# Split parts moved from GpSimd to VectorE ahead of layer 0, and an aggregation ordered by source tile

## What is computed

```python
h = maximum(layernorm(x), 0);  x1 = x + h              # x_in = h
g = batch_norm(h over the nodes) * bn_w + bn_b
g = gcn(g, gcn_in_w)      # out[d] = sum over edges s->d and s = d of (g @ W)[s] * dinv[s] * dinv[d]
for i in range(4):        # layers
    g = g + cross_attention(ln(g), cond, Wq, Wk, Wv, Wo)
    g = g + (val * gelu(gate)) @ ffo_w,  val, gate = split(ln(g) @ geglu_w)
g = gcn(g, gcn_out_w)
return x1 + g
```

## Time and profile before

| | |
|---|---|
| median of 3 runs | 2732.07 us |
| the profiled execution's own time | 2735.34 us |
| its span, first to last instruction | 2733.5 us |
| TensorE matmul busy | 2532.7 us, 93% |
| VectorE busy | 1371.1 us, 50% |
| ScalarE busy | 900.6 us, 33% |
| GpSimd busy | 762.6 us, 28% |
| first matmul of layer 0 | 364.14 us |
| share of the chain that ended last | PE 84%, DVE 10% |

### The profile page before, as it was taken

One profiled execution on the slowest core, in us unless ns is written; L12 is line 12 of the kernel. 1 busy time (PEld: TensorE's weight loads), 2 busy tenths in 40 slices (PEclk: granted clock), 3 DMA queues, 4 the chain that ended last, 5 costly groups with the idle time before them and its releaser, 6 DMA issues.

```text
span 2733.5 us, 34690 instructions
## 1 busy us (share of the span) xinstructions
PE 2532.7 (93%) x12399; PEld 2071.0 (76%) x12399; DVE 1371.1 (50%) x2852; ACT 900.6 (33%) x1735; POOL 762.6 (28%) x550
## 2 busy tenths in 40 slices
PE   2665779999999999999999999999999999999999
PEld 1231568888888788888888788888887888888887
DVE  9989636665222366663222566642223666622233
ACT  4132233335322133344222233352222333442211
POOL 4126220002544200015443000035442000154431
PEclk6576889999999999999999999999999999999999
DMA  3151331110221111111112011102111111011251
GB/s 130 43 219 77 138 128 38 56 77 16 77 64 67 74 62 62 36 47 64 65 66 96 32 62 61 47 31 78 62 65 63 62 62 77 16 62 62 69 205 68
DMA packets 39441, 197.48 MB, mean 72 GB/s; under 512 B 4112, under 2 KB 4496, under 8 KB 27024
## 3 DMA queue, kind: packets, MB, share of 16 engines
q1 hardware_dynamic: 39312, 195.81, 19.3%
HBM read 166.43 MB, written 29.36 MB: 72 GB/s over the span
## 4 chain that ended last, share of the span: by engine, by line
PE 84%; DVE 10%; issue 2%; DMA 1%; POOL 1%; ACT 1%; SPq 0%; POOLq 0%; ACTq 0%; DVEq 0%
PE ps L1286 25%; PE ps L1287 25%; PE ps L1288 25%; DVE oh_d L976 2%; PE ps L1449 2%; DVE oh_s L1015 2%; DVE oh_d L1017 2%; PE ps L1466 2%; PE ps L1468 2%; PE ps L1463 1%; DMA stage<-in_pieces 1%; DVE oh_s L974 1%; DVE z L1193 1%; PE ps L1490 1%; PE ps L1476 1%
## 5 line engine op out<-in xcount | busy, mean ns | idle before, releaser
L1286 PE MATMUL ps<-xT_hi,wg_hi 128*128 128x512 f32 (+1 forms) x1088 | 416.5, 383 | 0.0
L1287 PE MATMUL ps<-xT_lo,wg_hi 128*128 128x512 f32 (+1 forms) x1088 | 414.7, 381 | 0.0
L1288 PE MATMUL ps<-xT_hi,wg_lo 128*128 128x512 f32 (+1 forms) x1088 | 414.7, 381 | 0.0
L1240 DVE SCALAR_TENSOR_TENSOR ff<-ps,cols_sb,gel 128x512 f32<-128x512 f32 x128 | 96.1, 750 | 594.0 <-ACT gel L795 594.0
L795 ACT ACTIVATE gel<-ps,cols_sb 128x512 f32<-128x512 f32 x128 | 88.2, 689 | 637.9 <-PE ps L1288 637.8
L1249 DVE TENSOR_TENSOR h<-h,ps 128x512 f32<-128x512 f32 x256 | 175.6, 686 | 148.1 <-PE ps L1288 148.1
L1288 PEld LDWEIGHTS ps<-xT_hi,wg_lo 128*128 128x128 f32 x1088 | 209.8, 193 | 37.5
L1286 PEld LDWEIGHTS ps<-xT_hi,wg_hi 128*128 128x128 f32 x1088 | 210.0, 193 | 37.3
L1287 PEld LDWEIGHTS ps<-xT_lo,wg_hi 128*128 128x128 f32 x1088 | 209.7, 193 | 37.1
L413 POOL TENSOR_SCALAR veps<-mv 128x1 f32<-128x1 f32 x64 | 14.3, 223 | 793.2 <-DVE mv L853 793.2
L1286 PE MATMUL ps<-w_hi,cond_hi 128*128 128x512 f32 x512 | 202.5, 396 | 13.9 <-DMA cond_lo<-cond_lo_s 13.9
(11 more groups left out here) (222 smaller groups left out, 5352.6 us busy)
## 6 DMA issues: line engine op xcount, KB each, us to landing
stage<-in_pieces SPq DMA_DIRECT2D x138, 512.0 KB, 3.3
cond_hi<-cond_hi_s SPq DMA_DIRECT2D x34, 1024.0 KB, 4.8
cond_lo<-cond_lo_s SPq DMA_DIRECT2D x34, 1024.0 KB, 6.9
c_in<-in_condT SPq DMA_DIRECT2D x8, 1024.0 KB, 11.3
cond_hi_s<-cond_hi SPq DMA_DIRECT2D x8, 1024.0 KB, 4.2
cond_lo_s<-cond_lo SPq DMA_DIRECT2D x8, 1024.0 KB, 6.9
at_hi_s<-at_hi SPq DMA_DIRECT2D x1, 4096.0 KB, 13.1
at_lo_s<-at_lo SPq DMA_DIRECT2D x1, 4096.0 KB, 22.4
```

What stands on the lines that cost most here:

```text
L1240: dve.scalar_tensor_tensor(ff[:, s % 2, :], ps[:, step_bank(j, a, s, 0), :], cols_sb[:, bass.ds(COL["geglu_b"] + 32 * l + 4 * j + 2 * a + ...
L1286: pe.matmul(bank, l_hi, r_hi, start=(first and i == 0), stop=False)
L1287: pe.matmul(bank, l_hi, r_lo, start=False, stop=False)
L1288: end = pe.matmul(bank, l_lo, r_hi, start=False, stop=(last and i == n - 1))
```

## The change

It touches only what comes before layer 0, and the loop order of both aggregations.

1. `z1_of` uses SCALAR_TENSOR_TENSOR with x_rstd broadcast along the row as second tensor, not TENSOR_SCALAR.
2. `cond_low`, the first two `w_low` and the four `yT_lo` go from GpSimd to VectorE, between the codes: w_low behind chunks 14 and 17, yT_lo behind 26, 33, 40 and 47, cond_low(0) to (6) behind 51, 62, ..., 117, and cond_low(7) behind j = 12 of the second codes.
3. `xs_split(0, 1)` waits on GpSimd for the first digit of flush 0, the additions of the high digits stay there (flush 1), those of the low digits go to VectorE (`add_low`, between its `take_low` of flush 1).
4. The self loops come from TensorE: `open_sums(0)` has eight matmuls more, of a strip with a diagonal that VectorE writes once; the eight GpSimd additions L492 are gone.
5. Pieces 2 and 3 are copied by ScalarE between the digits of flush 0 and 1, and split by GpSimd when the last code is out; pieces 4 and 5 are loaded ahead of the stores, `at_hi` is stored alone, then pieces 6 and 7, `at_lo`, and pieces 8 and 9.
6. ScalarE does cond_high(2) to (5) ahead of the xs tiles, (6) in their middle and (7) behind them.
7. `aggregate` runs source by source over all eight targets for s = 0..3, and then target by target for s = 4..7.

```diff
+            for n in range(4, 6):
+                piece(n, n % 2)
+            sp.wait_ge(a_hi, NT)
+            sp.dma_start(at_s[0], ...at_hi...).then_inc(at_out, 16)
+            for n in range(6, 8):
+                piece(n, n % 2)
             sp.wait_ge(a_lo, NT // 2)
             sp.wait_ge(a_lo_odd, NT // 2)
-            for part, buf in zip(at_s, (at_hi, at_lo)):
-                sp.dma_start(part, bits(buf[:, :, :].rearrange("p t n -> p (t n)"))).then_inc(at_out, 16)
-            for n in range(4, FIRST_PIECES):
+            sp.dma_start(at_s[1], ...at_lo...).then_inc(at_out, 16)
+            for n in range(8, FIRST_PIECES):
                 piece(n, n % 2)
 # gpsimd
-            cond_low(0)
-            for n in range(2):
-                w_low(n, n, attn_place(0, 0, n), attn_place(1, 0, n))
-            for k in range(KC):
-                ...yT_lo[:, k, :]...
-            for g in range(1, GROUPS):
-                cond_low(g)
             pool.wait_ge(c_lo, GROUPS)
+            pool.wait_ge(a_digit, 1)
             xs_split(0, 1)
             for t in range(NT):
                 pool.wait_ge(a_digit, NT + t + 1)
                 pool.tensor_tensor(counts[:, t, HALF:N], counts[:, t, HALF:N], dig_h[:, t, :], ALU.add)
-                ...counts[:, t, 0:HALF] + dig_l[:, t, :]...
-                ...counts[:, t, own] + ident...
+            pool.wait_ge(oh_ok, CHUNKS + FLUSH * FLUSHES)
+            for n in range(2, 4):
+                w_low(n, n % 2, ...)
 # scalar
+            for g in range(2, 6):
+                cond_high(g)
             act.wait_ge(dinv_ok, 1)
-            for t in range(NT):
+            for t in range(4):
+                xs_of_g(t)
+            cond_high(6)
+            for t in range(4, NT):
+                xs_of_g(t)
+            cond_high(7)
...
             a_digits(0)
+            for n in range(2, 4):
+                w_high(n, n % 2, attn_place(0, 0, n % 2))
+            a_digits(1)
+            a_digits(2)
 # vector
-                dve.tensor_scalar(z1[:, t, :], x1[:, t, :], x_mv[:, t, 0:1], x_rstd[:, t:t + 1],
-                                  ALU.subtract, ALU.mult).then_inc(x0_ok, 1)
+                dve.scalar_tensor_tensor(z1[:, t, :], x1[:, t, :], x_mv[:, t, 0:1],
+                                         x_rstd[:, t:t + 1].broadcast_to([P, D]),
+                                         ALU.subtract, ALU.mult).then_inc(x0_ok, 1)
+            dve.memset(strip[:, 0:3 * P], 0.0)
+            dve.tensor_scalar(strip[:, 3 * P:], iota1[:, :], index[:, 0:1], None, ALU.is_equal)
+            dve.tensor_scalar(one_of[1], iota1[:, 0:P], index[:, 0:1], DIGIT, ALU.is_equal, ALU.mult)
             for c in range(CHUNKS):
                 scatter(c)
+                if c in (26, 33, 40, 47):
+                    y_low((26, 33, 40, 47).index(c))
+                if c in (14, 17):
+                    first_w_low((14, 17).index(c))
+                if c in range(51, 118, 11):
+                    cond_low((c - 51) // 11)
...
             for j in range(FLUSH * FLUSHES):
                 one_hots(j)
+                if j == 12:
+                    cond_low(7)
...
                     for t in range(NT):
                         take_low(j // FLUSH - 1, t)
+                        if j // FLUSH == 2 and t:
+                            add_low(t - 1)
 # tensor
-                    pe.matmul(ps[:, t, :], minus[:, :], shift[:, :], start=True, stop=True)
+                    pe.matmul(ps[:, t, :], minus[:, :], shift[:, :], start=True, stop=(f > 0))
+                    if f == 0:
+                        at = 3 * P - t % 4 * P
+                        pe.matmul(ps[:, t, :], one_of[t // 4], strip[:, at:at + HALF], start=False, stop=True)
 ...
+                for s in range(NT // 2):
+                    has(s)
+                    for t in range(NT):
+                        ...wait for bank t if s == 0...
+                        last = one(s, t)
+                last.then_inc(agg_half, 1)
+                for s in range(NT // 2, NT):
+                    has(s)
+                for t in range(NT):
+                    for s in range(NT // 2, NT):
+                        last = one(s, t)
+                    last.then_inc(agg_mm, 1)
```

More of the change, by code:

```diff
@@ L174, in gnn_preln_kernel @@
         pos_in = dig_h[:, 0:2, :].rearrange("p a (c n) -> p (a c) n", n=P)
+        strip = ind[:, :, :].rearrange("p b n -> p (b n)")[:, 0:HALF + 3 * P]
+        one_of = [ind[:, 3, :], ind[:, 7, :]]
         upto = dig_l[:, 0, :].bitcast(f16).rearrange("p (b n) -> p b n", n=P)
@@ L485, in _ @@
                     .then_inc(a_add, 1)
[L486 to L492, removed]
+            pool.wait_ge(oh_ok, CHUNKS + FLUSH * FLUSHES)
+            for n in range(2, 4):
+                w_low(n, n % 2, attn_place(0, 0, n % 2), attn_place(1, 0, n % 2))
             for t in range(0, NT, 2):
@@ L498, in _ @@
             zero_q()
-            for n in range(2, FIRST_PIECES):
+            for n in range(4, FIRST_PIECES):
                 w_low(n, n % 2, attn_place(0, (n - 2) // 2, n % 2), attn_place(1, (n - 2) // 2, n % 2))
@@ L655, in a_digits @@
                 fix(NT - 1)
-            for g in range(2, 6):
-                cond_high(g)
             for half in range(2):
@@ L876, in _ @@
             dve.tensor_copy(pay[:, 1, :], low_i[:, :]).then_inc(pay_ok, 1)
-            dve.wait_ge(iota_ok, 2)
-            dve.tensor_scalar(before[:, :], iota0[:, 0:P], index[:, 0:1], None, ALU.is_gt).then_inc(before_ok, 1)
+            dve.wait_ge(iota_ok, 3)
+            dve.tensor_scalar(before[:, :], iota1[:, 0:P], index[:, 0:1], None, ALU.is_gt).then_inc(before_ok, 1)
             def x_stats_of(half):
@@ L940, in _ @@
             dve.wait_ge(pos_ok, 6)
+            dve.memset(strip[:, 0:3 * P], 0.0).then_inc(strip_ok, 1)
+            dve.tensor_scalar(strip[:, 3 * P:], iota1[:, :], index[:, 0:1], None, ALU.is_equal).then_inc(strip_ok, 1)
+            dve.tensor_scalar(one_of[1], iota1[:, 0:P], index[:, 0:1], DIGIT, ALU.is_equal, ALU.mult)\
+                .then_inc(strip_ok, 1)
             def x_sum(t):
@@ L978, in scatter, with cond_low, first_w_low, y_low @@
                 last.then_inc(oh_ok, 1)
+            def cond_low(g):
+                s = g % 2
+                if g >= 2:
+                    dve.wait_ge(cond_out[s], 32 * (g // 2))
+                dve.wait_ge(c_hi, g + 1)
+                dve.tensor_tensor(cond_lo[s][:, :, :].rearrange("p k n -> p (k n)"), c_in[:, s, :],
+                                  bits(cond_hi[s][:, :, :].rearrange("p k n -> p (k n)")), ALU.subtract)\
+                    .then_inc(c_lo, 1)
+            def first_w_low(n):
+                dve.wait_ge(w_hi_ok, n + 1)
+                dve.tensor_tensor(attn_place(1, 0, n), stage[:, n, :], bits(attn_place(0, 0, n)), ALU.subtract)\
+                    .then_inc(w_ok, 1)
+            def y_low(k):
+                dve.wait_ge(y_hi, k + 1)
+                dve.tensor_tensor(yT_lo[:, k, :], full[:, :, :].rearrange("p a n -> p (a n)"),
+                                  bits(yT_hi[:, k, :]), ALU.subtract).then_inc(y_lo, 1)
             dve.wait_ge(pay_ok, 2)
@@ L1026, in take_low, with add_low @@
                 else:
-                    if f == 2:
-                        dve.wait_ge(a_add, 2 * t + 2)
                     dve.scalar_tensor_tensor(dig_l[:, t, :], dig_h[:, t, :], -DIGIT, ps[:, t, :],
                                              ALU.mult, ALU.add).then_inc(a_low, 1)
+            def add_low(t):
+                dve.wait_ge(a_low, NT + t + 1)
+                dve.tensor_tensor(counts[:, t, 0:HALF], counts[:, t, 0:HALF], dig_l[:, t, :], ALU.add)\
+                    .then_inc(a_acc, 1)
             def a_low_odd(t):
@@ L1046, in _ @@
                         take_low(j // FLUSH - 1, t)
+                        if j // FLUSH == 2 and t:
+                            add_low(t - 1)
+                    if j // FLUSH == 2:
+                        add_low(NT - 1)
             for t in range(NT):
@@ L1384, in aggregate, with one, has @@
             def aggregate(use):
-                for half in range(2):
+                def one(s, t):
+                    r = slice(t * P, (t + 1) * P)
+                    return product(ps[:, t, :], [(at_hi[:, s, r], at_lo[:, s, r], xs_hi[:, s, :], xs_lo[:, s, :])],
+                                   first=(s == 0), last=(s == NT - 1))
+                def has(s):
+                    if use:
+                        pe.wait_ge((xs_lo_ok, xs_lo_odd)[s % 2], (NT if s % 2 == 0 else 0) + s // 2 + 1)
+                    else:
+                        pe.wait_ge((a_lo, a_lo_odd)[s % 2], s // 2 + 1)
+                        pe.wait_ge(xs_lo_ok, s + 1)
+                for s in range(NT // 2):
+                    has(s)
                     for t in range(NT):
-                        r = slice(t * P, (t + 1) * P)
-                        if not half:
+                        if s == 0:
```

35 lines of the change are left out of this document (12 added, 23 removed).

## The result

The changed kernel takes **2689.81 us** (median of four runs, 2686.86 to 2692.53) against 2733.24 (2729.92 to 2734.66, four runs) for the kernel before beside it: ratio **0.9843, interval 0.9826 to 0.9860**, 43.4 us less. The forecast was 2690.5 with a range of 2678 to 2703. The profiled execution took 2686.86 us, its span is 2685.1.

A forecast was written before the change was run, and what follows sets the result against it. VectorE was taken to set the pace ahead of layer 0, then the SP queue. Parts of -2.2, +1.7, 0, -29.3 and -11.9 sum to -41.7 us, from 2732.07 to 2690.5; range 2678 to 2703.

The forecast's parts named there:

- A: Up to the first code: z1 +1.2, strip +0.75, wait behind cond_low(0) gone -4.15; sum -2.2 us.
- B: Up to chunk 96: VectorE subtractions +6.8, cond_low +11.0, waits +1.0, seven GpSimd instructions gone -17.1; sum +1.7 us.
- C: Chunks 96 to 127: TensorE rules, so cond_low(5) and (6) are covered; 0 us.
- D: The 135 second codes: 97.7 us instead of 127.0, so -29.3, with +12/-8.
- E: From at_hi complete (moment A) to layer 0: 37.5 us instead of 47.4, -9.9; granted clock another -2.
- the two-input row: L1051, VectorE reading two SBUF tensors: 0.68 us alone, 2.25 beside GpSimd's at_lo; z1's new form expected held likewise.
- Rival 3: Cond's loop in VectorE's queue makes codes wait for store, load and cond_high; slower, 2753 us at 18 per group; chance 0.04.
- more than 3 us: Sign of a wrong prediction: cond_low on VectorE waiting over 3 us in sum.
- the held codes: Second codes stretched beside GpSimd's xs_split and high additions: six per flush at 1.0 us each, 0 or 10 possible.
- add_low's meeting: In flush 1, VectorE's first add_low meets GpSimd's high-digit additions and is held by 1.0 us.
- Rival 2: Decodes give part back: GpSimd's 16 instructions 8, late cond queue 2, slow clock 4 us; 2700 as middle; chance 0.16.
- 30 us earlier: Sign expected in the trace: SP asks for cond 30 us earlier than in the kernel before.

The follow-up runs named there:

- the third experiment: The changed kernel with z1 back in its TENSOR_SCALAR form; 2687.13 us, first code at 37.31.
- The experiments on the high additions: Two edits of the changed kernel: GpSimd's eight high-digit additions left out, 2684.55 us; the same additions moved to VectorE, 2682.15 us.
- the second experiment: The changed kernel with the first half of the aggregation target by target again; 2684.91 us, layer 0 at 320.94.
- the last experiment: The changed kernel with old z1, d_low and d_high moved, aggregation's first half by target, high additions on VectorE, at_hi stored in halves; 2670.42 us, ratio 0.9762.
- the first experiment: The changed kernel with pieces 4 to 9 loaded only after both stores, as before; 2699.17 us, layer 0 at 333.91.
- the fifth experiment: The changed kernel with all eight cond_low back on GpSimd; 2706.14 us, layer 0 at 338.03.

## Why the prediction was right

By its own parts, in us. The first codes end at 157.70 before and 158.21 after, the last code of all at 286.0 and 254.6.

| Part | forecast | measured | reading |
|---|---|---|---|
| A, to the first code | -2.2 | -2.1 | 39.02 |
| B, to chunk 96 | +1.7 | +2.1 | product g at 129.28, as before |
| C, to the end of the first codes | 0 | +0.5 | 158.21 |
| D, the second codes | -29.3 | -32.0 | 96.4 for 128.3 |
| last code to A | 0 | -0.1 | 30.6 for 30.7 |
| E, A to layer 0 | -9.9 | -8.4 | A + 39.0 for A + 47.4 |
| sum to layer 0 | -39.7 | -40.0 | 324.16 |

**A.** z1 was held to 33.3 by d_low and d_high, as the two-input row had said; the third experiment shows the old form 1.7 ahead, not 1.2. The strip's three instructions took 0.44 us, not 0.75.

**B.** The waits for cond_high sum to 1.03 us (0.49 and 0.54, at chunks 84 and 95 as named), against 1.0 (0 to 3) in the sum. The price of 2.2 for a cond_low held (88.31 to 90.51), and the seven GpSimd instructions that are gone had cost 17.0, for 17.1. Of the 0.4 that B came out above its forecast these explain 0.1 to 0.2; the rest I can't place. Rival 3, in which the queue couldn't keep up, had its condition tested by the two waits alone: each group came 0.5 us late, not 6 or 9.

**C** was the one step that failed in its mechanism. I said that ScalarE's cond_high among the xs tiles delays only TensorE. cond_high(6) stands in ScalarE's queue behind four xs tiles, these wait for TensorE, and VectorE's cond_low(6) waits 2.42 us for it (147.33). TensorE ruled there, so it cost 0.5 us at the end; at chunk 60, where VectorE sets the pace, I would expect it to cost all. With this wait cond_low waits 3.45 us in sum, and the prediction had named more than 3 us as a sign of being wrong. By that sign it failed; the time hid it, as only 1.5 of the 3.45 reached the end of the first codes.

**D.** From the first code to the end of the last, the second codes take 95.2 us for the 97.7 of the sum. The term that was mis-sized is the held codes: five in each spot and not six, which is 2.0 of the 2.5 (the other 0.2 of the table is the stretch of before, 127.2 and not 127.0). Their price, 1.0 net, held. Two small terms were off against each other: add_low's meeting cost 1.6 us (1.1 + 0.5) and not 1.0, and the 1.13 us wait for TensorE behind the digits, which the sum has once for each flush, came only in the first (198.41), as add_low stands in its place in the second. That digits with a PSUM input are not held was right in both spots (eight in 4.86 us in the first). The experiments on the high additions show the held codes of the second spot by themselves.

**E.** Cond was asked for at A + 26.6 (26.5 forecast), and the split pieces are done at A + 33.9 (33.6). In the second experiment, where cond's load ends the wait, it ends at A + 34.9 (35.5). That the aggregation would be the last of the three was right too. Its end, A + 37.9, is the upper end of the span given. But that span isn't the sum of the terms it names: tile 7's digits at A - 4.1, 38.2 for the matmuls and 0 to 2.8 for the clock make A + 34.1 to 36.9, not 35.4 to 37.9. What was too low is the stretch at the slow clock: TensorE stood four times inside the first pass, and from 281.19 to 287.29 fourteen matmuls took 6.1 us for 3.2, so the clock cost 2.9 us, just above the 0 to 2.8. Rival 2's term of this name, the aggregation at the slow clock, came true at about half its price. GpSimd's sixteen instructions did not all meet codes. Three cond_low did wait, but 0.5 us above the allowed 1.0 is what it cost, not 2. As a sign, SP's request for cond "30 us earlier" was a slip: by the sum's own A + 26.5 it is 44, and 44.4 was measured (356.18 and 311.83).

It is luck that the errors nearly cancel: D gained 2.7 more than forecast, and B, C and E together 2.4 less (0.4, 0.5 and 1.5). The forecast of the time itself gained from the layers: the medians stand as if they had not changed, while the profiled pair alone would have said 48.

## What to carry to other kernels

A GpSimd instruction on SBUF tensors beside VectorE's TENSOR_SCALAR codes or its instructions with two SBUF tensors cost VectorE its own length here, less about 0.25 us. So price it by which of the two is quicker at the operation and not by who is free: here VectorE does the 128x2048 subtraction in 2.28 us and GpSimd in 4.5. Before moving such an instruction, list what VectorE has at its new place; if that is work with a PSUM input, as the digits here, or a reduction or statistics over one tensor, it costs nothing. When one wait is taken away, lay the other ends beside each other (aggregation A + 37.9, cond A + 34.9, pieces A + 33.9): here the order of a loop over PSUM banks was worth 3 us as soon as the load was no longer the last.

## What the runs showed of the hardware that I had not expected

A form with one SBUF tensor can be held as well: `before`, a 128x128 TENSOR_SCALAR in f16, took 7.03 us beside d_low and 0.25 alone. In the prediction I had two-input forms as the ones to look for. It isn't so for every such form. In the last experiment's kernel the TENSOR_REDUCE of 128x1024 took 1.94 us beside d_high, and 1.92 in the kernel after with GpSimd idle; the four BATCH_NORM_STATS2 took 2.47 beside d_low, and 2.48 with GpSimd idle. The TENSOR_SCALAR behind the reduction, `chunk`, was held for 3.14.

The granted clock of a stretch can be wrong in the records. These are the busy time and the granted clock (0.50 is 1.2 GHz, 1.00 is 2.4 GHz) of 129 to 132 us, in the kernel after and in the first experiment, and the matmuls of the kernel after in it.

```profile
129.00:132.00 3.00, 2.82 (x8) 1.00 1.01 426
```
```profile
129.00:132.00 3.00, 1.97 (x6) 0.50 0.97 401
```
```profile
129.28 0.77 PE L1316 MATMUL ps<-w_hi 128*128 128x512 f32 x1
129.84 0.63 PE L1317 MATMUL ps<-w_lo,w_hi 128*128 128x512 f32 x1
```
The matmuls come 0.43 us apart under a granted 1.00, as they do under 0.50 in the other trace. Three of the nine traces of changed kernels (the kernel after, and the third and the fifth experiment) show 1.00 up to about 158 us. The first codes end at 158.21 in the kernel after and between 158.96 and 159.56 in the four kernels that do the same work up to there and show less, 0.8 to 1.4 us later, of which 0.2 to 0.4 is there at the first code; before, with 0.50 in the record, they end at 157.70. So the 1.00 is no gain that these times show, and the pitch of the matmuls is the better witness of the clock.
